# A fused attention and expert layer: more buffers for the weight pieces that GpSimd splits beside the attention, and heads loaded one at a time

## The reference

```python
x = x + xattn(layernorm(x), pos, ctx)   # 16 heads of 32, causal, rotary, hidden size 512
x = x + ffn(layernorm(x))               # 8 experts of rank 16
# inside xattn, h = 512 x 4 residual streams:
qkv_in = rat_read(h, read_w, g, b, 3)                # mixes the 4 streams, layer norm per output
q, k, v = einsum("bli,oi->blo", qkv_in, qkv_w)
p = softmax(where(tril, rope(q) @ rope(k).T / sqrt(32), -1e30)); o = p @ v
h = rat_write(h, o, wod, wab, ...)                   # gates from softplus and exp
g_in, u_in = rat_read(h, mlp_read_w, ..., 2)
y = silu(g_in @ ctx[0].T) * (u_in @ ctx[1].T)        # 512 -> 2048, ctx is a weight of 2 x 2048 x 512
h = rat_write(h, y, mlp_wod, mlp_wab, ...)           # 2048 -> 632 columns
```

## Time and profile before

| | |
|---|---|
| median of three runs | 1709.99 us |
| the profiled execution's own time | 1711.99 us |
| its span, first to last instruction | 1710.2 us |
| PE busy | 1575.1 us, 92% |
| DVE busy | 1132.9 us, 66% |
| ACT busy | 906.5 us, 53% |
| POOL busy | 339.0 us, 20% |
| mean granted TensorE clock | 0.965 of full speed |
| moved by DMA | 364.29 MB, mean 213 GB/s |

### The profile page before, as it was taken

How to read it: one execution, slowest core, us unless ns; L and a number is a source line. 1 busy time by engine, 2 the same in 40 slices (tenths; PEclk the granted TensorE clock), 3 DMA queues, 4 the chain that set the end, 5 groups by cost and what they waited for, 6 DMA issues and landing times.

```text
span 1710.2 us, 24567 instructions
## 1 busy us (share of the span) xinstructions
PE 1575.1 (92%) x9238; PEld 1173.1 (69%) x9238; DVE 1132.9 (66%) x1758; ACT 906.5 (53%) x1672; POOL 339.0 (20%) x326
## 2 busy tenths in 40 slices
PE   7999999998889896789999899899899999999995
PEld 6565555665666563667799787698677788876653
DVE  7877755886778784924472764882865873546777
ACT  5333236886778673545462475552475733553453
POOL 1424533554433340020001210011100002000100
PEclk8999999999999998789999999999999999999998
DMA  9657567888988856356667766566766566665642
GB/s 354 217 201 297 181 172 213 249 243 223 246 216 208 209 173 243 110 192 228 230 188 214 241 211 235 165 230 211 245 224 240 181 214 199 225 212 180 222 178 99
DMA packets 129370, 364.29 MB, mean 213 GB/s; under 512 B 15954, under 2 KB 45266, under 8 KB 113892
## 3 DMA queue, kind: packets, MB, share of 16 engines
q1 hardware_dynamic: 128964, 362.59, 66.0%
q10 hardware_dynamic: 288, 0.13, 0.0%
HBM read 276.55 MB, written 86.11 MB: 212 GB/s over the span
## 4 chain that ended last, share of the span: by engine, by line
PE 68%; DVE 13%; ACT 6%; DMA 5%; SPq 3%; issue 3%; POOL 1%; DVEq 0%; ACTq 0%; POOLq 0%
PE ps L1609 20%; PE ps L1621 7%; PE ps L548 6%; PE ps L1634 4%; PE ps L1041 4%; PE ps L1028 3%; PE ps L1524 3%; PE ps L1552 3%; SPq L259 3%; PE ps L1064 3%; PE ps L1579 3%; PE ps L1567 3%; PE ps L1509 2%; DMA a_k<-qk_split 2%; ACT a_p L1143 2%
## 5 line engine op out<-in xcount | busy, mean ns | idle before, releaser
L1609 PE MATMUL ps<-m_y_split,m_win 128*128 128x512 f32 x1536 | 388.9, 407 | 8.4 <-issue 7.8
L1609 PEld LDWEIGHTS ps<-m_y_split,m_win 128*128 128x128 f32 x1536 | 287.6, 191 | 78.8 <-issue 14.0
L1085 DVE TENSOR_REDUCE a_negmax<-ps 128x1 f32<-128x640 f32 (+7 forms) x176 | 180.8, 1027 | 87.7 <-PE ps L1031 86.6
L1143 ACT ACTIVATE a_p<-ps,a_negmax 128x128 f32<-128x128 f32 (+7 forms) x256 | 188.6, 747 | 30.7 <-DVE a_negmax L1085 28.4
L1621 PE MATMUL ps<-m_wods,m_y_split 128*128 128x316 f32 x768 | 178.2, 320 | 0.9 <-DVE m_hT L1806 0.9
L1041 PE MATMUL ps<-ident,a_p 128*128 128x128 f32 x1152 | 162.4, 281 | 1.4 <-DVE a_pT L1098 1.2
L1028 PE MATMUL ps<-a_k,a_q 128*128 128x512 f32 (+3 forms) x384 | 128.8, 412 | 37.4 <-DMA a_k<-qk_split 19.5
L1844 ACT ACTIVATE m_turned<-ps 128x512 f32<-128x512 f32 x128 | 74.7, 595 | 132.8 <-PE ps L1509 123.4
L1041 PEld LDWEIGHTS ps<-ident,a_p 128*128 128x128 f32 x1152 | 128.0, 145 | 3.4 <-DVE a_pT L1098 1.9
L1621 PEld LDWEIGHTS ps<-m_wods,m_y_split 128*128 128x128 f32 x768 | 126.8, 189 | 3.8 <-issue 2.4
L1193 POOL TENSOR_SCALAR a_w_two<-a_w_raw 128x512 fp32r<-128x512 f32 (+1 forms) x64 | 79.9, 1248 | 206.8 <-DMA a_w_raw<-in_mlp_inT 112.1
(11 more groups left out here) (217 smaller groups left out, 2946.9 us busy)
## 6 DMA issues: line engine op xcount, KB each, us to landing
m_win<-mlp_in_split SPq DMA_DIRECT2D x128, 512.0 KB, 4.3
m_wods<-mlp_out_split SPq DMA_DIRECT2D x96, 316.0 KB, 3.3
m_wod<-in_wod1T SPq DMA_DIRECT2D x64, 316.0 KB, 2.9
p_xT<-in_xT SPq DMA_DIRECT2D x16, 1024.0 KB, 9.5
p_x<-in_x SPq DMA_DIRECT2D x16, 1024.0 KB, 10.5
a_q<-qk_split SPq DMA_DIRECT2D x64, 256.0 KB, 6.7
a_k<-qk_split SPq DMA_DIRECT2D x128, 128.0 KB, 7.0
mlp_in_split<-a_w_two SPq DMA_DIRECT2D x32, 512.0 KB, 3.1
```

Of the source, the lines that this page charges most:

```text
L1085: V.tensor_reduce(negmax[:, n % 4, 0:len(units[n][3])], by_head(n, score_banks(n)), AX_X, ALU.max, negate=True).then_inc(max_ready, 1)
L1143: m = S.activation(dst[:, j, :], src[:, j, :], ACT.Exp, bias=negmax[:, n % 4, j:j + 1], accum_out=rsum[:, si % 2, q * 4 + hh:q * 4 + hh + 1])
L1609: m = nc.tensor.matmul(bank_of("m", blk, step), win[s][:, wl, ic, :], y[k], start=(ic == 0 and p3 == 0), stop=(ic == HCH - 1 and p3 == 2))
```

## The change

Four things are changed, all in the attention stage.

- Loaded pieces have four buffers in place of two, and results three in place of two. The new ones lie in ring slots 3 and 4 of the next stage.
- `load_raw` runs three pieces ahead in place of one. SP starts with three loads, and loads piece u + 3 where it loaded u + 1.
- The heads of the next four are loaded one at a time at units 2, 3, 4 and 5 of a four, the values with the last of them, in place of all at unit 3.
- The last piece is stored at unit `NU - 8` in place of `NU - 4`. The two ring slots that held the new buffers are loaded only when all pieces are done and stored.

```diff
@@ the ring slots
             w2s.append(sb(f"m_wods{k}", [P, 2, HALFW], F32R))
+            place[0] = start
+            if k == NW - 2:
+                w_raw += [sb(f"a_w_raw{i}", [P, HCH * P]) for i in (2, 3)]
+            elif k == NW - 1:
+                w_two.append(sb("a_w_two2", [P, 2, HCH * P], F32R))
+            assert place[0] <= end
             place[0] = end
...
-        raw_loaded, two_stored, two_ready = sems("raw_loaded", 2), sems("two_stored", 2), sem("two_ready")
+        raw_loaded, two_stored, two_ready = sems("raw_loaded", 4), sems("two_stored", 3), sem("two_ready")
...
+        def stored_before(u, s):
+            return 16 * sum(1 for v in range(u) if v % 3 == s)
@@ attend_pool
-                    s, w = u % 2, piece_width(u)
-                    pool.wait_ge(raw_loaded[s], 16 * (u // 2 + 1))
-                    pool.wait_ge(two_stored[s], 16 * (u // 2))
+                    r, s, w = u % 4, u % 3, piece_width(u)
+                    pool.wait_ge(raw_loaded[r], 16 * (u // 4 + 1))
+                    pool.wait_ge(two_stored[s], 16 * (u // 3))
@@ attend_sp
             def load_raw(u):
                 if u < PIECES:
-                    sp.wait_ge(two_ready, u - 1)
+                    sp.wait_ge(two_ready, u - 3)
...
-            load_raw(0)
+            for u in range(3):
+                load_raw(u)
             for n, (si, u) in enumerate(beside):
-                if n < NU and si % 3 == 0 and u == 3 and sets[si][0] + 1 < fours:
+                if n < NU and si % 3 == 0 and u in (2, 3, 4, 5) and sets[si][0] + 1 < fours:
                     f4 = sets[si][0] + 1
-                    for h in range(4):
-                        load_head(4 * f4 + h)
-                    load_v(f4)
+                    load_head(4 * f4 + u - 2)
+                    if u == 5:
+                        load_v(f4)
...
                 for u in pieces_at(n):
                     if u:
                         store_two(u - 1)
-                    load_raw(u + 1)
-                if n == NU - 4:
-                    store_two(PIECES - 1)
+                    load_raw(u + 3)
...
                 if n == NU - 8:
+                    store_two(PIECES - 1)
                     for k in range(NW):
+                        if k == NW - 2:
+                            sp.wait_ge(two_ready, PIECES)
+                            for s in range(3):
+                                sp.wait_ge(two_stored[s], stored_before(PIECES, s))
                         load_weights(k)
```

More of the change, by code:

```diff
@@ L1189, in attend_pool @@
                 for u in pieces_at(n):
-                    s, w = u % 2, piece_width(u)
-                    pool.wait_ge(raw_loaded[s], 16 * (u // 2 + 1))
-                    pool.wait_ge(two_stored[s], 16 * (u // 2))
-                    m = pool_own.then_inc(G.tensor_scalar(w_two[s][:, 0, 0:w], w_raw[s][:, 0:w], 1.0, None, ALU.mult))
+                    r, s, w = u % 4, u % 3, piece_width(u)
+                    pool.wait_ge(raw_loaded[r], 16 * (u // 4 + 1))
+                    pool.wait_ge(two_stored[s], 16 * (u // 3))
+                    m = pool_own.then_inc(G.tensor_scalar(w_two[s][:, 0, 0:w], w_raw[r][:, 0:w], 1.0, None, ALU.mult))
                     pool.wait_ge(pool_own.sem, m)
-                    G.tensor_tensor(w_two[s][:, 1, 0:w], w_raw[s][:, 0:w], w_two[s][:, 0, 0:w].bitcast(F32),
+                    G.tensor_tensor(w_two[s][:, 1, 0:w], w_raw[r][:, 0:w], w_two[s][:, 0, 0:w].bitcast(F32),
                                     ALU.subtract).then_inc(two_ready, 1)
@@ L1239, in load_raw @@
                 if u < PIECES:
-                    sp.wait_ge(two_ready, u - 1)
+                    sp.wait_ge(two_ready, u - 3)
                     k, r = divmod(u - 2 * MCH, 2)
                     piece = mlp_inT[u] if u < 2 * MCH else wod2T[k][:, HALFW * r:HALFW * r + HALFW]
-                    move(w_raw[u % 2][:, 0:piece_width(u)], piece).then_inc(raw_loaded[u % 2], 16)
+                    move(w_raw[u % 4][:, 0:piece_width(u)], piece).then_inc(raw_loaded[u % 4], 16)
             def store_two(u):
@@ L1247, in store_two @@
                 to = win_d[u] if u < 2 * MCH else wod2_d[u - 2 * MCH]
-                move(to, w_two[u % 2][:, :, 0:piece_width(u)]).then_inc(two_stored[u % 2], 16)
+                move(to, w_two[u % 3][:, :, 0:piece_width(u)]).then_inc(two_stored[u % 3], 16)
             def store_o(si):
@@ L1284, in attend_is_over @@
                 e.wait_ge(oT_stored[s], oT_count[NSETS - 2 + s])
-                e.wait_ge(two_stored[s], 16 * (PIECES // 2))
+            for s in range(3):
+                e.wait_ge(two_stored[s], stored_before(PIECES, s))
         def prepare_sp():
@@ L1467, in load_weights @@
                 u = 2 * mc + g2
-                sp.wait_ge(two_stored[u % 2], 16 * (u // 2 + 1))
+                sp.wait_ge(two_stored[u % 3], 16 * (u // 3 + 1))
                 move(win[s][:, :, :, :].rearrange("p a c m -> p a (c m)"), win_d[u]).then_inc(wt_loaded[s], 16)
```

## The result

The changed kernel takes 1684.5 us (median of four runs, 1682.9 to 1690.0) against 1711.6 us before on the same chip: a ratio of 0.9846, 95% interval 0.9821 to 0.9870. Run again later, beside other kernels, it took 1684.6 us (0.9835, 0.9818 to 0.9852). The profiled execution has a span of 1682.1 us, 28.1 less than before.

What follows compares the result with a forecast made beforehand. PE is busy 92% of the span; late heads, behind SP waiting for GpSimd, cost waits and clock. The profiled 1711.99 us less 26 is 1686, for the median 1684, with 1 us of losses 1685; own range 1681 to 1690, overall 1678 to 1699.

Steps and rivals of the forecast that it cites:

- The price of late heads: Attention: PE's waits for late heads plus lower clock cost four fours 8.30, 4.41, 5.69 and 8.07 us, together 26.5.
- the mean of 43.2: Attention: mean of three stretches without a wait for heads (42.78, 43.38, 43.49 us), the level excesses were taken over.
- The cause: Attention: SP, held by GpSimd's pieces, takes 44.2 to 51.3 us from block to block, longer than the 43.2 needed.
- The hole that a deeper prefetch fills: Attention: behind a block of head loads GpSimd idles 19.10 us and SP issues nothing; pieces loaded ahead would fill this.
- The lead needed: Attention: head loads must begin some 22 us before their four as a block, 26 to 28 one at a time.
- A turn of 38 to 40 us if unheld, a lead near 38: Attention: with new buffers SP's turn falls under 43.2 us, blocks start some 5 us into the four, all excesses go.
- DMA share of 0.91 in the wide fours: Attention's first four stretches: DMA share without the excess is 0.91 against 1.06 for a full queue, so transfers fit.
- Three loads ahead and three results: Attention: three pieces in hand cover 8.3 us of GpSimd work; three result buffers let it finish them without a store.
- Costs of 0 at the start and the end: Attention: two extra first loads, bounds 0 and 0.9 us, and the last store's 3.5 us wait, covered by 16 us.
- GpSimd beside DVE: Attention: the same GpSimd work in a shorter stage slows DVE, at most 0.6 us a four, 4 in all.
- 1685 from 26 us less: Whole kernel: 26 us less gives 1684 for the median, with 1 us for losses 1685; chance 0.80.
- upper bound of 29: Attention: high end of the gain, 29 us, if every four takes the 42.78 us of the fastest.

## Why the prediction was right

- **The price of late heads** (26.5 us as an excess of four stretches): right. These fours gave 28.6 us. The difference is that the undisturbed level is 42.7 to 42.8 us and not the mean of 43.2 that I took; 43.3 is reached only by the four that also has the constants.
- **The cause** (SP's turn is longer than a four, and GpSimd's pieces hold SP): right. Longer pieces lengthen the turn and bring the waits back, and an earlier place without a shorter turn lasts two fours.
- **The hole that a deeper prefetch fills** (19.1 us): only in part right. It is still 15 us long. Loads are in hand, but the results that GpSimd has finished wait for their stores, which stand behind the heads. The first piece behind the block begins 28.4 us after the block (361.25 to 389.69) and not 24; the 15.0 us from there to the next block are the five or six pieces that I counted.
- **The lead needed** (22 us for a block, 26 with a piece step in it): the first agrees with every run: blocks 21.8 us ahead or more had no wait for a head, and at 21.2 or less all had one. One by one, 26 and 28 were too much. With doubled work of GpSimd two fours had 24.7 us and lost nothing, 24.4 cost 0.7 and 22.6 brought a wait of 0.9; in the run with the heads alone 23.6 cost 0.6.
- **A turn of 38 to 40 us if unheld, a lead near 38**: the turns are 40.8 to 43.4 except the last, which the constants (4.1 us of issues) lengthen to 46.8; SP does keep pace. The lead is 32 to 36. I had the block start 5 us into a four; it starts 8 to 10 us into it in the first fours, since GpSimd's hole of 15 us remains, and 7.1 us into the fifth and the sixth. It was enough.
- **DMA share of 0.91 in the wide fours**: mis-sized. It is 1.02, 1.01, 1.00 and 0.91 in the first four stretches. My sum kept the bytes of each stretch, but SP is no longer behind, so the pieces come earlier: 12.1 MB fall into the second four (42.78 us at 284 GB/s) and not 11.0, and less into the last (0.43). It did no harm, since a head has 33 us.
- **Three loads ahead and three results**: right that both count, though I priced them together. Loads alone give 11 to 12 us, results alone nothing, both 27 to 28. Heads one by one give 9 to 10 us alone and nothing on top.
- **Costs of 0 at the start and the end**: right. The weights went out at 601.84 us for 617.50.
- **GpSimd beside DVE** (at most 4 us): nothing that shows. The stretch with 24.12 us of GpSimd's work has 37.49 us of DVE's and is 42.78 us long, no longer than its neighbours, and the experiment with doubled work agrees.
- **1685 from 26 us less**: the attention gave 31.0, five more than the sum and two more than its upper bound of 29, and 2.9 were given back behind it at a lower clock, which the sum did not have. The two nearly cancel; that the median of 1684.5 lies so close to 1685 is luck.

## What to carry to other kernels

Compare the length of a queue's own turn with the period that its consumer needs: if the turn is longer, loads drift late however early they stand, and moving them only buys a credit that is soon used up. The cure is to cover the longest hold of the queue's program at both ends, here with two buffers more for loads and one more for results: the results alone gave nothing, the loads alone less than half of what both gave. After moving a block of loads, look at what stands behind it in the queue: small constants behind 4.5 MB held DVE for 11.2 us and through it PE for 11.6, though neither had anything to do with the move.

## What the runs showed of the hardware

- All 16 DMA engines can be full for three fours in a row (shares of 1.02, 1.01 and 1.00, 280 to 288 GB/s), while PE and ACT are busy as long as before to 0.1 us, and no stretch is longer than 42.79 us. DVE's busy time moves between 36.6 and 37.5 us.
- Full engines are no fixed rate here. While heads land they move 224 GB/s. Two stretches of 4 us of the changed kernel, heads landing and then weight pieces and attention output; last columns: clock, DMA share, GB/s:

```profile
334.00:338.00 4.00, 4.00 (x41) 3.09 (x41) 3.36 (x5) 3.65 (x10) 2.44 (x2) 1.00 1.06 233
346.00:350.00 4.00, 4.00 (x39) 2.61 (x38) 3.18 (x5) 3.98 (x9) 0.94 (x1) 1.00 1.05 412
```

  The transfers of heads are 64 and 32 partitions wide and the others 128; no run separates the width from the other differences between them.
- Traces with the same program for PE behind the attention, and the same waits of PE to 3 us, differ there by up to 4.8 us. Between the kernel before and the changed one it is 2.9, and what differs is the clock that PE was granted.
